# First tile's rows by selecting matmuls, and an opening in another order, in a DLRM tower with three cross layers (Trainium2, one core)

## The reference

```python
e = jnp.stack([tbl_0[ids[:, 0]], ..., tbl_38[ids[:, 38]]], axis=1)   # 512 x 39 x 16
xk = x0 = e
for W in (f0, f1, f2):              # (39*39, 128), (128*39, 128), (128*39, 128)
    z = jnp.einsum('bfd,bgd->bfgd', x0, xk).reshape(b, f * g, d)
    xk = jnp.einsum('bpd,pm->bmd', z, W)          # kept as one of three outputs
result = jnp.sum(jnp.concatenate(outs, axis=1), axis=-1)
h = jnp.concatenate([result, dense_ctx], axis=1)
h = jnp.maximum(h @ W_top1 + b_top1, 0.0)
h = jnp.maximum(h @ W_top2 + b_top2, 0.0)
y = h @ W_top3
```

## Time and profile before

| what | us |
|---|---|
| median of 3 runs (653.37 to 654.81) | 654.61 |
| the profiled execution | 655.92 |
| its span, first to last instruction | 653.9 |
| TensorE busy in the span | 623.1 |
| first layer-1 matmul of block 0 starts at | 27.41 |
| first layer-1 matmul of block 1 starts at | 76.25 |

### The profile page before, as it was taken

How to read it: one execution, slowest core, us unless ns; L and a number is a source line. 1 busy time by engine, 2 the same in 40 slices (tenths; PEclk the granted TensorE clock), 3 DMA queues, 4 the chain that set the end, 5 groups by cost and what they waited for, 6 DMA issues and landing times.

```text
span 653.9 us, 12272 instructions
## 1 busy us (share of the span) xinstructions
PE 623.1 (95%) x2653; PEld 485.2 (74%) x2653; DVE 539.6 (83%) x1221; ACT 539.7 (83%) x1881; POOL 491.4 (75%) x459
## 2 busy tenths in 40 slices
PE   0788899999999999999999999999999999999998
PEld 0466578888888888888888888888888888875673
DVE  0668779989898989898989889898989898998870
ACT  1446588989898989898989989898989898987762
POOL 5887879889898979898989898898988754241430
PEclk9989989999999999999999999999999999999999
DMA  8336432322223131223132313223230320402000
GB/s 219 66 72 125 118 81 44 69 56 53 71 40 84 16 90 28 75 45 80 42 83 43 82 42 63 61 53 71 38 87 10 91 72 1 115 1 75 4 0 1
DMA packets 65502, 40.32 MB, mean 62 GB/s; under 512 B 37486, under 2 KB 50480, under 8 KB 65482
## 3 DMA queue, kind: packets, MB, share of 16 engines
q1 hardware_dynamic: 54201, 35.37, 22.9%
q0 software_dynamic: 5184, 1.29, 2.2%
q10 hardware_dynamic: 6097, 3.44, 2.1%
HBM read 38.13 MB, written 1.94 MB: 61 GB/s over the span
## 4 chain that ended last, share of the span: by engine, by line
PE 88%; issue 4%; DVE 3%; ACT 2%; SPq 2%; DMA 1%; ACTq 0%; DVEq 0%
PE psa L935 13%; PE psa L931 13%; PE psa L932 13%; PE psd L931 8%; PE psd L935 8%; PE psd L932 8%; PE psg L905 5%; PE ps L869 4%; PE ps L868 4%; PE ps L870 3%; PE psg L999 1%; PE psg L993 1%; DVE cur L603 1%; DVE parts L632 1%; ACT parts L754 1%
## 5 line engine op out<-in xcount | busy, mean ns | idle before, releaser
L754 ACT ACTIVATE parts<-psa,x0c 128x128 f32<-128x128 f32 x1536 | 449.2, 457 | 60.5 <-PE psa L935 48.5
L632 DVE SCALAR_TENSOR_TENSOR parts<-psd,x0c,parts 128x128 f32<-128x128 f32 x960 | 266.2, 344 | 56.5 <-PE psd L935 50.4
L603 DVE TENSOR_REDUCE cur<-parts 128x64 f32<-128x1536 f32 x128 | 223.7, 1749 | 6.5 <-DVE parts L632 2.5
L931 PE MATMUL psa<-w1h,x1h 128*128 128x512 f32 x384 | 169.0, 440 | 3.4 <-ACT parts L754 2.8
L424 POOL TENSOR_TENSOR z0l<-pairs,z0h 117x512 fp32r<-117x512 f32 (+1 forms) x98 | 127.0, 1304 | 43.8 <-ACT z0h L707 43.1
L935 PE MATMUL psa<-w1h,x1l 128*128 128x512 f32 x384 | 152.8, 398 | 2.6 <-issue 2.6
L932 PE MATMUL psa<-w1l,x1h 128*128 128x512 f32 x384 | 151.6, 395 | 0.0
L405 POOL DMA_INDIRECT emb<-tables,idx x130 | 126.5, 973 | 23.9 <-issue 23.8
L414 POOL TENSOR_TENSOR pairs<-x0t,pairs 117x512 f32<-117x512 f32 (+1 forms) x98 | 127.0, 1305 | 1.7 <-DMA x0t<-x_rows 1.1
L931 PE MATMUL psd<-w1h,x1h 128*128 128x512 f32 (+1 forms) x256 | 100.8, 394 | 1.1 <-DVE parts L632 1.1
L935 PE MATMUL psd<-w1h,x1l 128*128 128x512 f32 (+1 forms) x256 | 97.6, 381 | 0.0
(11 more groups left out here) (106 smaller groups left out, 569.9 us busy)
## 6 DMA issues: line engine op xcount, KB each, us to landing
pairs<-x_rows SPq DMA_DIRECT2D x105, 156.0 KB
pairs<-x_rows SPq DMA_DIRECT2D x30, 234.0 KB
x0t<-x_rows SPq DMA_DIRECT2D x45, 78.0 KB
gram<-w ACTq DMA_DIRECT2D x3, 832.0 KB, 7.8
emb<-tables,idx POOLq DMA_INDIRECT x130
pairs<-x_rows_first SPq DMA_DIRECT2D x8, 136.5 KB
x_rows<-emb SPq DMA_DIRECT2D x13, 72.0 KB
wt_sb<-w_top SPq DMA_DIRECT2D x1, 768.0 KB, 6.3
```

Of the source, the lines that this page charges most:

```text
L603: return dve.tensor_reduce(cur1[:, t % 2, first:end], terms[:, first:end, :, :], AX.XY, ALU.add)
L632: op = dve.scalar_tensor_tensor(acc, y[:, M * j:M * j + M], x0c[:, t, GF * g + j:GF * g + j + 1], acc, ALU.mult, ALU.add)
L754: op = act.activation(lanes(dst, j), y[:, M * j:M * j + M], ACT.Copy, scale=x0c[:, t, GF * g + j:GF * g + j + 1])
L931: pe.matmul(y[:, 0:n], hi, w1h[:, c], start=True, stop=False)
```

## The change

1. **Tile 0 of block 0 goes no longer through DRAM.** POOL gathers its rows, DVE spreads each gather's 16 numbers over 8 masked copies (`space_rows`), three matmuls with a 0/1 matrix `selectors` put them in the shape of `x0t` in PSUM, ACT copies that out, and seven matmuls with a 0/1 matrix `shifts` make the shifted rows, which DVE multiplies straight out of PSUM (`z0_of_opening`).
2. **Fillers.** `stay_awake(n)`: n matmuls of 359 columns whose result nobody reads: 8 at the start, 1 after the selection, 1 after `first_tile(0)`. The 4 matmuls of L951 go.
3. **Block 0's rows lie in `gram`** (`first_pairs`, `first_x0t`), no longer in `pairs` and `x0t`. So block 1's rows are loaded without waiting for block 0's layer 0.
4. **Two DRAM scratches** for the blocks' rows, used in turn.
5. **W1 and W2 are stored so that each partition's run is one piece**; W1 comes in 6 pieces (`W1_CUTS`) with their own semaphores. Pieces 2 to 5 are issued after tile 0's gathers have landed; their splits into `w1h` and `w1l` stand between the groups of tile 0.
6. **ACT waits for the ids before its first DMA.** Identity, mask and biases are issued by SP. 10 gathers in place of 12 for block 0: the last features of two tiles share one. SP writes tiles 2 and 3 before it loads them.
7. **The tables** place block 1's layer 0 and `w0l` elsewhere.

```diff
-L0_AT_FIRST = {(2, 8): [0], (3, 0): [1], (3, 2): [2], (3, 4): [3], (3, 5): [4], (3, 7): [5], (3, 8): [6]}
+L0_AT_FIRST = {(2, 4): [0], (2, 7): [1], (2, 8): [2], (3, 3): [3], (3, 5): [4, 5], (3, 7): [6]}
...
-SECOND_Z0_AT = {(2, 0): [0, 1], (2, 1): [2], (2, 2): [3, 4], (2, 3): [5, 6]}
+SECOND_Z0_AT = {(1, 3): [0, 1], (2, 0): [2], (2, 1): [3], (2, 2): [4], (2, 3): [5, 6]}
...
+WARMING, BETWEEN = 8, 1
+W1_CUTS = [0, 4, 8, 16, 24, 32, F]
+W1_FIRST = 2
+W1_AHEAD = 4
+W0L_AT_FIRST = (1, 1)
...
+    scratch = [nc.dram_tensor(f"x0_rows{i}", (F + SHIFTS, BB, D), F32, kind="Internal").ap() for i in range(2)]
...
             def load_rows(b):
                 sp.wait_ge(scr_written, 16 * SCR_DMAS * b)
                 for i, (first, end) in enumerate(PIECES):
 
-                    sp.wait_ge(l0_steps, L0T * (b - 1) + end)
+                    if b > 1:
+                        sp.wait_ge(l0_steps, L0T * (b - 1) + end)
...
+            def space_rows(c):
+                n = 128 if c < TCH - 1 else TLAST
+                dve.wait_ge(gathered_opening[c], 16)
+                if c == 0:
+                    dve.wait_ge(sel_in, 16)
+                dve.tensor_tensor(spaced[0:n, c, :].rearrange("p (b d) -> p b d", d=D),
+                                  emb_tiles[0:n, c, :].unsqueeze(1).to_broadcast([n, TB, D]),
+                                  sel_sb[0:n, 0:TB].unsqueeze(2).to_broadcast([n, TB, D]),
+                                  ALU.mult).then_inc(spaced_ready, 1)
...
+            def z0_of_opening():
+                dve.wait_ge(x0t_opening, 1)
+                for i, (first, end) in enumerate([(0, 4), (4, L0T - 1)]):
+                    dve.wait_ge(shifted, i + 1)
+                    op = dve.tensor_tensor(first_pairs[0][0:ROWS, first:end, :],
+                                           psd[i][0:ROWS, 0:128 * (end - first)].rearrange("p (k n) -> p k n", n=128),
+                                           first_x0t[0][0:ROWS, :].unsqueeze(1).to_broadcast([ROWS, end - first, 128]), ALU.mult)
...
+            act.wait_ge(ids_in, 16)
             act.dma_start(w0s[0:ROWS, :, :], w0a).then_inc(w0_in, 16)
...
+            for i in range(W1_PIECES):
+                if i == W1_FIRST:
+                    for landed in gathered_opening:
+                        act.wait_ge(landed, 16)
+                c = slice(W1_CUTS[i] * M, W1_CUTS[i + 1] * M)
+                act.dma_start(w1raw[:, c], w1[:, c]).then_inc(w1_in[i], 16)
...
+            def stay_awake(n):
+                for _ in range(n):
+                    pe.matmul(psa[A_RING - 1][:, 0:SELECTORS], sel_sb[:, 0:128], sel_sb, start=True, stop=True)
...
+            def opening_rows():
+                for c in range(TCH):
+                    n = 128 if c < TCH - 1 else TLAST
+                    at = TB + ROWS * c
+                    pe.wait_ge(spaced_ready, c + 1)
+                    op = pe.matmul(psg[0:ROWS, 0:TB * D], sel_sb[0:n, at:at + ROWS], spaced[0:n, c, :],
+                                   start=(c == 0), stop=(c == TCH - 1))
+                op.then_inc(placed, 1)
+                stay_awake(BETWEEN)
+                pe.wait_ge(shift_in, 16)
+                pe.wait_ge(x0t_opening, 1)
+                for k in range(L0T):
+                    op = pe.matmul(psd[k // 4][0:rows_of(k), 128 * (k % 4):128 * (k % 4) + 128],
+                                   shift_sb[:, ROWS * k:ROWS * k + rows_of(k)], first_x0t[0][0:F, :], start=True, stop=True)
+                    if k in (3, L0T - 1):
+                        op.then_inc(shifted, 1)
```

More of the change, by code:

```diff
@@ L87 @@
 HIGH_AT = {(2, 3): 0, (3, 1): 1, (3, 4): 2}
[L88 removed]
+HIGH_AT_FIRST = {(3, 5): 0}
 LOW_AT = {(2, 3): 0, (3, 1): 1, (3, 3): 2}
@@ L118, in turn, with tile_column, w1_piece @@
     return sum(on_pool(i) == pool for i in range(f + 1))
+def tile_column(t, c):
+    return 5 * (t // 2) + (c if t % 2 == 0 or c == 2 else 3 + c)
+def w1_piece(f):
+    return sum(at <= f for at in W1_CUTS[1:-1])
 def rows_of(k):
@@ L540, in _ @@
             for t in range(TILES):
-                for c in range(TCH):
+                for c in range(TCH if t % 2 == 0 else TCH - 1):
                     gather_tile(t, c)
@@ new lines, in w1_low, with w0_low @@
+            def w1_low(k):
+                c = slice(W1_CUTS[k] * M, W1_CUTS[k + 1] * M)
+                dve.wait_ge(w1h_ready, k + 1)
+                dve.tensor_tensor(w1l[:, c], w1raw[:, c], w1h[:, c].bitcast(F32), ALU.subtract).then_inc(w1l_ready, 1)
+            def w0_low():
+                split_w0 = w0s[0:ROWS, SPLIT[0]:SPLIT[-1] + 1, :].rearrange("p t m -> p (t m)")
+                dve.wait_ge(w0h_ready, 1)
+                dve.tensor_tensor(w0l[0:ROWS, :], split_w0, w0h[0:ROWS, :].bitcast(F32), ALU.subtract).then_inc(w0l_ready, 1)
@@ L661, in _ @@
             dve.tensor_tensor(w0s[0:ROWS, :, :], w0s[0:ROWS, :, :], w0braw[0:ROWS, :, :], ALU.add).then_inc(w0_summed, 1)
[L662 to L665 removed]
+            for c in range(TCH):
+                space_rows(c)
             w1_low(0)
[L668 to L671 removed]
+            z0_of_opening()
             w1_low(1)
             low_part(0, 0)
[L674 removed]
+            for i in range(2, W1_AHEAD):
+                w1_low(i)
             block_of(0, True, slice(BB, 2 * BB))
@@ L733, in scalars, with w1_high @@
                 act.activation(x0c[:, t, 0:F], pst[:, ROWS * t:ROWS * t + F], ACT.Copy).then_inc(x0c_ready, 1)
+            def w1_high(k):
+                c = slice(W1_CUTS[k] * M, W1_CUTS[k + 1] * M)
+                act.wait_ge(w1_in[k], 16)
+                act.activation(w1h[:, c], w1raw[:, c], ACT.Copy).then_inc(w1h_ready, 1)
             def gram_out(T, at):
@@ L803, in _ @@
             act.activation(w0h[0:ROWS, :], split_w0, ACT.Copy).then_inc(w0h_ready, 1)
+            w1_high(0)
+            act.wait_ge(placed, 1)
+            act.activation(first_x0t[0][0:ROWS, :], psg[0:ROWS, 0:TB * D], ACT.Copy).then_inc(x0t_opening, 1)
             w1_high(1)
             scalars(0, 0)
+            w1_high(2)
             high_part(0, 0)
-            w1_high(2)
+            for i in range(3, W1_AHEAD):
+                w1_high(i)
             block_of(0, True, True)
@@ L945, in block_of @@
                             grams(T - 1, (t - 1) % TILES)
+            pe.wait_ge(sel_in, 16)
+            stay_awake(WARMING)
+            opening_rows()
+            pe.wait_ge(ident_in, 16)
             pe.wait_ge(w0_summed, 2)
-            pe.wait_ge(first_written[0], 16 * FIRST_WRITES)
-            for _ in range(WARMING):
-                pe.matmul(ps0[:, :], w0s[0:ROWS, 0, :], w0s[0:ROWS, 0:4, :].rearrange("p t m -> p (t m)"), start=True, stop=True)
-            pe.wait_ge(ident_in, 16)
             first_tile(0)
+            stay_awake(BETWEEN)
             block_of(0, True)
@@ L1041, with by_gather @@
     base = np.repeat(first_row.reshape(CH, FPC).T, BB, axis=0)
-    tile_ids = np.concatenate([arr["ids"][:BB], arr["ids"][:BB, 0:TCH * TFPC - F]], axis=1)
-    tile_ids = tile_ids.reshape(TILES, TB, TCH, TFPC).transpose(3, 1, 0, 2).reshape(128, TGATHERS)
-    tile_row = np.zeros(TCH * TFPC, np.int32)
-    tile_row[:F] = start
-    tile_base = np.tile(np.repeat(tile_row.reshape(TCH, TFPC).T, TB, axis=0), (1, TILES))
+    def by_gather(rows):
+        wide = np.concatenate([rows, rows[:, 0:1]], axis=1).reshape(TILES, TB, F + 1)
+        halves = [wide[:, :, TFPC * c:TFPC * c + TFPC].transpose(0, 2, 1).reshape(TILES, 128) for c in range(TCH - 1)]
+        ends = wide[:, :, TFPC * (TCH - 1):F].transpose(0, 2, 1).reshape(TILES // 2, 2 * TLAST)
+        ends = np.concatenate([ends, ends[:, 0:128 - 2 * TLAST]], axis=1)
+        columns = []
+        for t in range(0, TILES, 2):
+            columns += [halves[0][t], halves[1][t], ends[t // 2], halves[0][t + 1], halves[1][t + 1]]
+        return np.stack(columns, axis=1)
+    tile_ids = by_gather(arr["ids"][:BB])
+    tile_base = by_gather(np.tile(np.asarray(start, np.int32), (BB, 1)))
     f_of = np.arange(SPT * L0T * F).reshape(SPT * L0T, F) % F
@@ L1073 @@
         "identity": np.eye(ROWS, dtype=np.float32),
+        "selectors": selectors.astype(np.float32),
+        "shifts": shifts.astype(np.float32),
     }
```

208 lines of the change are left out of this document (118 added, 90 removed).

## The result

| | kernel before | changed |
|---|---|---|
| median | 653.99 us (653.37 to 654.81, 4 runs) | 642.46 us (642.27 to 643.57, 4 runs) |
| profiled execution | 655.92, span 653.9 | 642.27, span 640.4 |
| block 0's first layer-1 matmul | 27.41 | 20.87 |
| block 1's first layer-1 matmul | 76.25 | 64.05 |
| from there to the end of the span | 577.65 | 576.35 |

Ratio 0.982, 95% interval 0.9804 to 0.9836: 11.5 us faster. 645.9 was forecast, with rival A, the wait for block 1's rows gone, at 643. The two profiled executions differ by 13.65, more than the medians, since the profiled one of before lies 1.9 over its median.

The account below looks back on a forecast made before the run. TensorE bounds the steady part (36.80 of 36.80 us busy), so only time before block 1 can be won. Block 1's first layer-1 matmul moves from 76.25 to 67.5: 654.6 - 8.7 = 645.9 us, range 642.0 to 650.5.

Parts of the forecast that it names:

- rival A: Before block 1: its rows land before 43, DVE does not wait, POOL's list is next; gain 11.5, 643 us; chance 0.22.
- Ids at 3.1: Opening: the ids' DMA takes 2.3 us, so POOL's addition comes at 3.1, 2.7 us earlier (bounds 0 to 3.4).
- Copy at 14.8 behind `w0h` and `w1h`: Opening: ACT copies tile 0's selected rows at 14.8, its queue order behind DMA issues and splits costing 2.6 us.
- Layer 1 at 20.6, with the clock fallen: End of opening: block 0's layer 1 starts at 19.1 at 2.4 GHz, or 20.6 with 1.5 added for the fallen clock.
- DVE reaches block 1's products at 42.7 to 44.2: Block 0, end of tile 1: DVE gets to block 1's products at about 42.7, or 44.2 with the low clock.
- Tiles 1 to 3 of block 0 loaded before DVE asks for them: Block 0: loads come at about 22, 29, 31, before DVE asks (24, 30, 36); delays up to 5 us are swallowed.
- Block 1's rows at 47.0: Before block 1's products: rows land at 47.0 (bounds 44.5 to 49), so DVE idles 3 to 4 us.
- POOL 5.2 earlier: POOL's gathers for block 1's rows end 5.2 us earlier, at 34.9 for 40.06, by ids (2.7) and two fewer gathers.
- From the products 20.5 us to block 1: DVE's products, sum and tiles 2 and 3 run from 47.0 until block 1's first layer-1 matmul at about 67.5.
- From block 1 on only a shift: After block 1's start: the same work in the same order, so nothing but a shift.
- W2, two scratches, three more DMAs on SyncE at nothing: W2's longer runs, the second DRAM scratch and SP's three extra DMAs (about 0.45 each) were costed at nothing.
- Rival C: Before block 1's products: slower if rows land from 55.7 on; at 58 the time would be 656.5; chance 0.05.

Follow-up runs that it names:

- the first profile: The first profiled execution of the unmodified changed kernel: 642.27 us, span 640.4, with block 1's first layer-1 matmul at 64.05.
- experiment 10: Changed kernel with W1 and W2 back in the earlier layout, runs of 512 bytes, same pieces and places: 644.98 us, ratio 0.9869.
- experiment 2: Changed kernel with four fillers in place of one behind the selection, to hold TensorE's clock: 642.73 us, ratio 0.9834.
- c0: Profile of the unmodified changed kernel run again in the first group of experiments: execution 642.94 us; that run's median 642.69 us, ratio 0.9839.
- experiments 3 and 4: experiment 3, and the changed kernel with block 1's loads waiting again for block 0's layer 0: the latter 643.65 us, ratio 0.9852.
- c2: Profile of the unmodified changed kernel run again as control in the third group of experiments: median 642.8 us, ratio 0.9831.
- experiment 11: Changed kernel with one DRAM scratch for all blocks' rows, writes waiting again for the block before's loads: 642.35 us, ratio 0.9821.
- experiment 8: Changed kernel with later VectorE products of block 1, four fillers behind the selection, POOL's tile 2 products ahead of its last three gathers: 659.27 us, ratio 1.0028.
- the second group: Four variants of the changed kernel run on one chip beside the kernel before, which took 657.75 us there (654.37 to 661.27).
- experiment 3: Changed kernel without ACT's wait for the ids, so ids share the DMA engines with w0 again: 643.86 us, ratio 0.986.

## Why the forecast was right in direction and range, and 3.4 us short

The chain of the forecast is the right one, but its main wait was mis-sized, so that the result lies with rival A. The forecast's own sign for A, no idle time of DVE before L676, is what the first profile shows.

- *Ids at 3.1*: 2.80. Right. *Copy at 14.8 behind `w0h` and `w1h`*: 14.26. Right, and experiment 10 shows how tight that queue is.
- *Layer 1 at 20.6, with the clock fallen*: 20.87 and 20.65, once 22.14. Right; experiment 2 shows 19.30 with the clock held, as the other end of the forecast had it (19.1).
- *DVE reaches block 1's products at 42.7 to 44.2*: 43.43 and 44.54 without a wait, 42.73 in c0. Right.
- *Tiles 1 to 3 of block 0 loaded before DVE asks for them*: nearly. Tile 2's rows came 0.24 us late in c0, and with an earlier layer 1 tiles 1 and 2 came 0.82 and 0.56 late (experiment 2). The forecast expected a late load to be swallowed by the wait for block 1's rows; in c0 it was.
- *Block 1's rows at 47.0*: **this step failed.** In c0 they let DVE go at 44.82, in the first profile by 43.43. The terms: POOL's last gather 33.05 (30.54 + 0.92 = 31.46 in the first profile) where 34.9 was forecast; it landed 2.45 later (35.50; 2.59 in the first profile), not 3.7; the writes' landing took 1.7 for 2.0; against that, x0t took 3.7 after its issue in place of 2.65. That is 1.85 + 1.2 + 0.3 - 1.05, less 0.1 on the issues, the 2.2 us between 47.0 and 44.82. The landing of 3.7 had been taken from before.
- *POOL 5.2 earlier*: it was 8.6 (first profile) and 7.0 (c0). The ids gave 3.0 for 2.7 and the two gathers 2.5 as forecast. Another 1.3 us in c0 come from block 0's gathers, of which two were stretched before (1.42 and 2.21 us for 0.95) and one, by 0.4, in c0. In block 1's ten gathers the stretching that the forecast kept (3.9 us) was still there in c0 (3.8 us), and 2.1 in the first profile.
- *From the products 20.5 us to block 1*: 20.38 in c0, 20.39 in experiments 3 and 4, 20.62 in the first profile. Right. So the failed step passes into block 1's start: 65.2 for 67.5 in c0, and 64.05 in the first profile, where the rows did not bind at all.
- *From block 1 on only a shift*: 1.3 us shorter (1.75 in c0). Before, TensorE idled 1.49 and 0.29 at 81.6 and 82.9 and then ran passes of 0.63 for 0.40 up to 86.3; after, the waits at the same place are 1.54 and 0.30, or 0.89, and no such passes follow. The forecast had seen no clock there. It is not the whole cause: in c2 the granted clock fell at this place too (0.50 from 72 us), and the stretch was still 1.1 us shorter than before.
- *W2, two scratches, three more DMAs on SyncE at nothing*: experiment 11, and POOL's wait for W2's split of 7.85 us against 7.86. Right. **The layout of W1 was not costed at all**: its 2 us were part of the sum only because the four issues were entered with 0.46 each.
- The sum: forecast 8.7 from profile to profile, measured 13.65, of which 12.2 are block 1's start, 1.3 what follows it and 0.15 outside the span. On its own terms the forecast was thus 4.95 us short. That the time was only 3.4 off is in part luck: it booked a saving read from a profile 1.3 over the median on the median itself, which gave 1.3 back, and the profiled execution of the changed kernel lies 0.2 under its median.
- *Rival A* is what the first profile shows, in time (643) and in mechanism: no wait for rows, DVE's work on block 0 done so that block 1 begins at 64.05 (about 64), and then POOL's list next, with ScalarE's first group at 68.17 (about 69). In other executions it is a mixture: in c0 and experiments 2 to 4 the wait for rows is there with 1.3 to 2.1 us. Its words "takes the low end of three bounds at once" are what happened to two of them.
- *Rival C's "656.5" for a landing at 58* should read about 657 by its own terms (58 - 55.7 = 2.3 over 654.6); nothing rests on it.

On the rule of the Trainium skill, page "SBUF — State Buffer", section "Who interferes with whom", which infers that a tensor_tensor on SBUF leaves descriptor writing alone: c0's ten gathers of block 1 contain 1.96, 2.94 and 1.73 us where the others take 0.94, and DVE splits W1 (L653) and multiplies in SBUF in that stretch. In experiment 8 VectorE stood still from 17 to 32 us, and all ten took 0.92 to 0.97:

```profile
20.82 0.94 POOL L450 DMA_INDIRECT emb_first<-tables,idx_first  x1 [0.30 <-issue]
20.84 2.37 DVE L653 TENSOR_TENSOR w1l<-gram,w1h 128x1024 fp32r<-128x1024 f32 x2
22.07 1.96 POOL L450 DMA_INDIRECT emb_first<-tables,idx_first  x1 [0.30 <-issue]
24.33 2.94 POOL L450 DMA_INDIRECT emb_first<-tables,idx_first  x1 [0.30 <-issue]
27.57 1.73 POOL L450 DMA_INDIRECT emb_first<-tables,idx_first  x1 [0.30 <-issue]
```

```profile
21.61 0.95 POOL L450 DMA_INDIRECT emb_first<-tables,idx_first  x1 [0.30 <-issue]
```

(c0 first, then one gather of experiment 8.) Gathers are stretched where VectorE works and not where it stands still, which speaks against the inference but does not settle it. ScalarE stood still in the same stretch of experiment 8, so the two engines are not told apart; and c0's gather of 20.82 ran beside L653 for its whole 0.94 us, so such an operation does not stretch every gather. No run changed VectorE's work alone.

## What to carry to other kernels

A start that waits for the later of two chains gains only up to the second: price both to their landings before adding up what the first one saves (here 1.35 us of earlier layer 1 bought nothing, and 1 us of later rows moved block 1 by 1). When the first wait is gone, look for the next: here the rows of tiles 1 and 2, those of block 1 and POOL's list all stood within 2 us. Whatever stands in an engine's queue ahead of a short critical copy is on the path, DMA issues with many short runs above all. And a transfer's landing read from one stretch is no constant for another: the gathers landed 2.45 us after the last one's issue where 3.7 had been read, x0t 3.7 where 2.65 had been. Such a term needs a range, in both directions.

## What was not expected of the hardware

- On the chip of the second group, in the profiles of all four kernels, ScalarE and VectorE stood still for 5 to 17 us between 16 and 39 us though what they wait for, by the trace, had long ended. TensorE's transpose had ended at 17.3 in experiment 8, and ScalarE's timeline goes on at 32.5:

```profile
16.95 0.32 PE L974 MATMUL pst<-ident_sb,gram 117*128 117x117 f32 x1
...
32.54 0.20 ACT L821 ACTIVATE x0c<-pst 128x39 f32<-128x39 f32 x1 [16.90 <-remote]
```

SyncE's issues came up to 1.4 us apart there, many of them 0.7; POOL's gathers ran on at their usual pace, and no instruction packet moved on the DMA queues from 15 to 45 us. Layer 1 began 14 to 19 us later than on the other chips and these variants of the changed kernel had medians of 657 to 665 us, about those of the kernel before or over them. Not every execution was that long: without fillers, four of twelve took 653.4 to 654.9. The kernel before took 4 us more there than elsewhere, and its own profile on the first chip has such gaps on three engines, of 2.55 (TensorE), 2.36 (ScalarE) and 1.88 us (VectorE), between 37 and 44 us. The cause stays open, and so does what the unmodified changed kernel does on that chip: it was not among the four. Whether it is the chip or the time of the runs can't be told from one group. The gain of some 11 us holds in the other groups (11.5, 10.9 and 11.1).
- The clock of TensorE fell to the 1.2 GHz level behind an idle of 1.6 us (0.50 from 16 to 22 us) although TensorE had been busy from 3.88 to 13.06 us; with the idle filled (experiment 2), or with the selection so late that none was left (experiment 3), it did not. An idle time of that length does not always do it: near block 1's start the clock fell to 0.50 behind 1.49 us in the kernel before and 1.47 in c2, and stayed at 1.00 behind 1.54 in the first profile.
